# A GRU over four lanes with gathered gate rows: the candidate's input rows in a bank of their own, split products for two lanes, and the transposed embedding kept from the table stage

## The chip, the cores and the metric

The kernel runs on one core of a Trainium2 chip. The metric is the device time of the program in microseconds (us), lower is better; three runs of the kernel before took 1370.25, 1371.12 and 1375.16 us.

## What is computed

A GRU with hidden size H = 128 runs over T = 50 tokens for each of B = 2048 sequences, and the state at each sequence's last position is multiplied with the transposed embedding table (V = 12501 rows of 128), which gives the logits, 2048 x 12501 in f32.

```python
xp = jnp.einsum('bth,hk->btk', emb_table[input_ids], kernel) + b_i
rec = h @ rec_kernel + b_r
z = sigmoid(xz + rz); r = sigmoid(xr + rr)
hh = tanh(xh + r * rh)
h_new = z * h + (1.0 - z) * hh
logits = last @ emb_table.T
```

## The kernel before

**Table stage.** The product of an embedding row with the input weights depends on the token alone. So the kernel first makes a table in DRAM, `gate_table`, with 384 values (z, r and candidate parts) for each of the 12501 tokens. It goes over 24 chunks of 512 embedding rows and a rest of 213. For each chunk SyncE (SP) loads the rows into a slot of `emb_rows` (L239), TensorE (PE) turns them (L349) into `x_ps`, ScalarE (ACT) copies the high part as f32r (L528), VectorE (DVE) subtracts for the low part (L641), PE makes three f32r products for each of the four 128-row tiles (L369 to L371) into the banks of `z_ps` and `r_ps`, DVE and ACT copy them out (L650, L537), and SP stores them (L234). Each partition takes four neighbouring rows of a chunk, so that it reads 2048 and writes 6144 bytes in one piece. DVE also works out row numbers for all tokens in this stage; positions behind a sequence's last go to a row that freezes the state.

**Recurrence.** The batch is four lanes of 512 sequences. The state is kept transposed, [128 hidden, 512 sequences]. A step g takes one block (a whole lane of 512, or half of lane 3, 256 wide) through one token. There are three phases, all in groups of four steps: phase one, 100 steps on lanes 0 and 1 in turn; phase two, 100 steps, in turn a whole step on lane 2 and a half step on a half of lane 3; phase three, 50 half steps on the two halves of lane 3. Block g+2 goes on where block g ended.

GpSimd (POOL) gathers the table rows of each tile of 128 sequences with one indirect DMA (L335), four steps ahead, into the buffer that step g-4 has left. On PE a step (`step`, L409) turns the gathered rows of the r gate into `r_ps` (L399), adds the f32 product with the state (L406, two matmul instructions for one product), makes the candidate's product into `c_ps`, turns and adds for z into `z_ps`, and, after DVE has multiplied `c_ps` by r in place, adds the turned candidate rows to it. Each of the three has two banks and `x_ps` the other two. ACT (`gate`) takes r's sigmoid (L562), z's sigmoid (L564) and the candidate's tanh (L568). DVE (`update`) does (c + bias) * r in PSUM (L765), z * h (L768), (z - 1) * candidate (L772) and the new state (L775).

**What fills the gaps.** In phase one, once in four steps, SP loads a chunk of the embedding again, this time with row p of a tile on partition p (L268), PE turns it (`vocabulary`), ACT and DVE split it into `embT_hi` and `embT_lo` (L575, L780). In phases two and three every step carries two units of the logits of lanes that are done: a unit is 128 sequences by 512 vocabulary columns, three f32r products (L457, L458, L459) into one of two banks of `x_ps`. ACT copies a unit out (L586) and SP stores it. In a half step both units stand on PE behind z's product and both copies on ACT before the tanh. In a whole step the first unit stands there, the second behind the candidate's rows, and both copies behind the tanh. A unit waits until the copy of the unit before it in its bank is done (L452). At the end PE makes the units of lane 3, with ACT and DVE copying in turn (L614, L813), through `x_ps` and `z_ps`.

The order of each engine is written out by hand: four programs with `wait_ge` on counting semaphores, run in order.

Of the kernel before, what the change touches and what calls it, by code (L numbers as in the profile page):

```python
# [22 lines left out]
def gru_logits(nc, ids, mask, emb, w_in, w_rec, bias, out):  # L23
# [58 lines left out]
    def tiles_of(blk):  # L82
        return blk[2] // P
# [4 lines left out]

    def gathers(k, q):

        return sum(16 * tiles_of(phase_of(j)[q]) for j in range(k))
# [5 lines left out]
    with ExitStack() as ctx:  # L97
# [14 lines left out]
        w_rec_sb = sb("w_rec_sb", [P, G])  # L112
        bias_sb = sb("bias_sb", [P, 2, 3])
# [20 lines left out]
        z_sb, r_sb, cand = gates[:, 0], gates[:, 1], gates[:, 2]  # L134

        table_rows = gates[:].rearrange("p a b c -> p (a b c)").rearrange("p (k n g) -> p k n g", k=2, n=TPC)
        rowsT_hi = state_hi[:, 2:4]
        rowsT_lo = state_lo[:, 2:4]
# [10 lines left out]
        z_ps = psum("z_ps", [P, SETS, BANK])  # L149
        r_ps = psum("r_ps", [P, SETS, BANK])  # L150
        c_ps = psum("c_ps", [P, SETS, BANK])
        x_ps = psum("x_ps", [P, 2, CHUNK])
# [9 lines left out]
        s_w_in_parts = sem("s_w_in_parts")  # L162
        s_math = sem("s_math")
# [12 lines left out]
        s_turned = sem("s_turned")  # L176
        s_rec = sem("s_rec")
# [3 lines left out]
        s_scaled = sem("s_scaled")  # L181
        s_cand = sem("s_cand")
# [6 lines left out]
        s_rows = sem("s_rows")  # L189
        s_rowsT = sem("s_rowsT")  # L190
        s_hi = sem("s_hi")
        s_lo = sem("s_lo")
# [14 lines left out]
        def emb_chunk(chunk):  # L207

            return emb[bass.ds(chunk * CHUNK, CHUNK), :].rearrange("(n p) h -> p n h", p=P)
# [7 lines left out]
        def _(sp):  # L217
# [44 lines left out]

            sp.wait_ge(s_rowsT_ps, FULL + 1)
            for j, m in RAGGED:
                sp.dma_start(emb_rows[0:m, 0, j, :], emb[ragged_rows(j, m), :]).then_inc(s_rows, 16)
            for k in range(1, K2 - 1):
                sp.wait_ge(s_rowsT, k)
                sp.dma_start(emb_rows[:, 0], emb_chunk(k - 1)).then_inc(s_rows, 16)  # L268
            sp.wait_ge(s_rowsT, K2 - 1)
            sp.dma_start(emb_rows[:, 0], emb_chunk(K2 - 2)).then_inc(s_rows, 16)  # L270
# [39 lines left out]
        def _(pool):  # L310
# [32 lines left out]
        def _(pe):  # L343
            pe.wait_ge(s_ident, 1)

            def turn_rows(bank, slot, tiles):

                for j, m in tiles:
                    turned = nc.tensor.transpose(x_ps[:, bank, j * P:j * P + m], emb_rows[0:m, slot, j, :],  # L349
# [10 lines left out]
            def project(c, k, tiles=WHOLE, first=False):  # L360
# [487 lines left out]
```

## Time and profile before

| | us |
|---|---|
| median of 3 runs (lowest, highest) | 1371.12 (1370.25, 1375.16) |
| the profiled execution, its own time | 1370.22 |
| its span, first to last instruction | 1368.1 |
| PE busy | 1180.8 (86%) |
| POOL busy | 784.2 (57%) |
| DVE busy | 692.4 (51%) |
| ACT busy | 686.6 (50%) |

Busy time is summed over the span and says nothing of where a stage waits. The page names as the chain that ended last mostly PE's products with the state (r 12%, c 11%, z 10%) and, with 11%, "another core or an unknown queue". There is one core only: the profile says this where a semaphore rose long after the recorded end of the instruction that raises it, and other views call it "remote". Ends of matmuls are modelled.

### The profile page before, as it was taken

How to read it: one execution, taken by the hardware profiler on the slowest of the kernel's cores; microseconds unless marked ns; L12 is line 12 of the kernel's file. 1: busy time of each engine (PE TensorE's matmuls, PEld its weight loads, DVE VectorE, ACT ScalarE, POOL GpSimd, SP SyncE). 2: the span in 40 equal slices, each digit the busy share in tenths (PEclk: the TensorE clock that was granted, in tenths of full speed). 3: DMA queues.
4: the chain of work that ended last, by engine and by line, in shares of the span. 5: the costliest groups of instructions: out<-in, count | busy, mean ns of one | idle time of the engine just before them, and what ended most of it. 6: DMA issues, size and time to landing. Idle time of an engine off the chain costs nothing.

```text
span 1368.1 us, 16235 instructions
## 1 busy us (share of the span) xinstructions
PE 1180.8 (86%) x5590; PEld 795.3 (58%) x5590; DVE 692.4 (51%) x1191; ACT 686.6 (50%) x1203; POOL 784.2 (57%) x812
## 2 busy tenths in 40 slices
PE   7947778777878778778799999999999999999998
PEld 7933444343444334444466666666666668888776
DVE  7624455444545445445554555545555555444554
ACT  3522333333433333333456666666666667777644
POOL 0027667666776767667666666666666655555200
PEclk9979898888988888989999999999999999999999
DMA  8965555555555555555467887777887778888799
GB/s 292 366 179 153 142 152 146 147 152 141 154 146 148 146 154 146 148 143 159 132 196 239 260 254 253 250 238 253 256 261 253 237 249 269 285 282 284 239 365 333
DMA packets 127489, 294.21 MB, mean 215 GB/s; under 512 B 18096, under 2 KB 33456, under 8 KB 127408
## 3 DMA queue, kind: packets, MB, share of 16 engines
q0 software_dynamic: 51200, 157.34, 39.3%
q1 hardware_dynamic: 76208, 135.84, 29.6%
q8 instruction: 45, 0.74, 0.2%
q14 instruction: 36, 0.29, 0.1%
HBM read 171.30 MB, written 121.81 MB: 214 GB/s over the span
## 4 chain that ended last, share of the span: by engine, by line
PE 67%; another core or an unknown queue 11%; DVE 6%; ACT 6%; issue 5%; DMA 4%; POOL 0%; SPq 0%; DVEq 0%; ACTq 0%; POOLq 0%
PE r_ps L406 12%; PE c_ps L406 11%; PE z_ps L406 10%; PE x_ps L457 6%; PE x_ps L459 5%; PE x_ps L458 5%; PE c_ps L399 5%; PE r_ps L399 4%; PE z_ps L399 3%; DVE c_ps L765 2%; DMA gate_table<-gates 2%; ACT gates L562 2%; ACT gates L564 1%; DMA out_dram<-logits 1%
## 5 line engine op out<-in xcount | busy, mean ns | idle before, releaser
L335 POOL DMA_INDIRECT gathered<-gate_table,index x800 | 782.3, 978 | 495.9 <-issue 204.1
L564 ACT ACTIVATE gates<-z_ps,zr_bias 128x512 f32<-128x512 f32 (+1 forms) x250 | 151.6, 607 | 329.7 <-PE z_ps L406 162.7
L768 DVE TENSOR_TENSOR kept<-gates,state 128x512 f32<-128x512 f32 (+1 forms) x250 | 147.2, 589 | 237.5 <-ACT gates L564 192.0
L406 PE MATMUL r_ps<-state,w_rec_sb 128*128 128x512 f32 (+1 forms) x500 | 256.6, 598 | 0.0
L772 DVE SCALAR_TENSOR_TENSOR gates<-gates 128x512 f32<-128x512 f32 (+1 forms) x250 | 146.1, 585 | 209.0 <-issue 125.4
L399 PE MATMUL c_ps<-ident,gathered 128*128 128x128 f32 x800 | 116.4, 260 | 145.7 <-DVE c_ps L765 125.2
L406 PE MATMUL c_ps<-state,w_rec_sb 128*128 128x512 f32 (+1 forms) x500 | 235.1, 554 | 0.0
L406 PE MATMUL z_ps<-state,w_rec_sb 128*128 128x512 f32 (+1 forms) x500 | 233.8, 550 | 0.0
L399 PEld LDWEIGHTS c_ps<-ident,gathered 128*128 128x128 f32 x800 | 92.0, 144 | 232.6 <-DVE c_ps L765 180.7
L765 DVE SCALAR_TENSOR_TENSOR c_ps<-c_ps,bias_sb,gates 128x512 f32<-128x512 f32 (+1 forms) x250 | 162.0, 648 | 126.2 <-PE c_ps L406 47.2
L562 ACT ACTIVATE gates<-r_ps,zr_bias 128x512 f32<-128x512 f32 (+1 forms) x250 | 151.0, 604 | 143.3 <-PE r_ps L406 56.6
L586 ACT ACTIVATE logits<-x_ps,nan_row 128x512 f32<-128x512 f32 (+1 forms) x300 | 194.4, 683 | 20.0 <-PE x_ps L459 14.1
L568 ACT ACTIVATE gates<-c_ps,bias_sb 128x512 f32<-128x512 f32 (+1 forms) x250 | 150.3, 601 | 90.6 <-PE c_ps L399 51.8
L399 PE MATMUL z_ps<-ident,gathered 128*128 128x128 f32 x800 | 187.5, 349 | 0.0
L457 PE MATMUL x_ps<-embT_hi,state_hi 128*128 128x512 f32 (+1 forms) x350 | 176.4, 504 | 5.7 <-DVE state_lo L752 1.6
L775 DVE TENSOR_TENSOR state<-kept,gates 128x512 f32<-128x512 f32 (+1 forms) x250 | 148.6, 594 | 26.7 <-DVE gates L772 0.9
L399 PEld LDWEIGHTS z_ps<-ident,gathered 128*128 128x128 f32 x800 | 101.3, 147 | 103.6 <-issue 93.6
L406 PEld LDWEIGHTS c_ps<-state,w_rec_sb 128*128 128x128 f32 x500 | 104.1, 208 | 92.3 <-issue 86.9
L458 PE MATMUL x_ps<-embT_lo,state_hi 128*128 128x512 f32 (+1 forms) x350 | 137.1, 392 | 0.0
L459 PE MATMUL x_ps<-embT_hi,state_lo 128*128 128x512 f32 (+1 forms) x350 | 136.5, 390 | 0.0
L399 PE MATMUL r_ps<-ident,gathered 128*128 128x128 f32 x800 | 111.6, 256 | 18.7 <-DMA gathered<-gate_table,index 18.7
L399 PEld LDWEIGHTS r_ps<-ident,gathered 128*128 128x128 f32 x800 | 88.7, 145 | 26.0 <-issue 19.4
(78 smaller groups left out, 870.8 us busy)
## 6 DMA issues: line engine op xcount, KB each, us to landing
out_dram<-logits SPq DMA_DIRECT2D x192, 512.0 KB, 4.7
gate_table<-gates SPq DMA_DIRECT2D x24, 768.0 KB, 4.1
gathered<-gate_table,index POOLq DMA_INDIRECT x800
emb_rows<-in_L_rec_emb_table_dram SPq DMA_DIRECT2D x48, 256.0 KB, 4.6
out_dram<-logits SPq DMA_DIRECT2D x8, 213.0 KB, 3.9
logits<-in_r_input_ids_dram SPq DMA_DIRECT2D x1, 400.0 KB, 6.1
logits<-in_r_input_mask_dram SPq DMA_DIRECT2D x1, 400.0 KB, 6.5
gate_table<-gates SPq DMA_DIRECT2D x2, 192.0 KB, 9.2
```

Of the source, the lines that this page charges most:

```text
L335: nc.gpsimd.indirect_dma_start(gathered[:, q, n, :].bitcast(F32), None, table, bass.IndirectOffsetOnAxis(ap=index[:, g, n:n + 1], axis=0)) ...
L399: turned = nc.tensor.matmul(bank[:, n * P:(n + 1) * P].bitcast(F32R), gathered[:, q, n, gate * H:(gate + 1) * H], ident[:], is_transpose=T ...
L406: return nc.tensor.matmul(bank, w_rec_sb[:, gate * H:(gate + 1) * H], h, start=first, stop=True, skip_group_check=True)
L457: nc.tensor.matmul(bank[:, 0:even], high, embT_hi[:, bass.ds(v0, even)], start=True, stop=False)
L458: nc.tensor.matmul(bank[:, 0:even], high, embT_lo[:, bass.ds(v0, even)], start=False, stop=False)
L459: nc.tensor.matmul(bank[:, 0:even], low, embT_hi[:, bass.ds(v0, even)], start=False, stop=True).then_inc(s_unit, 1)
L562: nc.scalar.activation(r_sb[:, b, 0:width], r_ps[:, b, 0:width], ACT.Sigmoid, bias=zr_bias[:, 1:2]).then_inc(s_r, 1)
L564: nc.scalar.activation(z_sb[:, b, 0:width], z_ps[:, b, 0:width], ACT.Sigmoid, bias=zr_bias[:, 0:1]).then_inc(s_z, 1)
L568: nc.scalar.activation(cand[:, b, 0:width], c_ps[:, b, 0:width], ACT.Tanh, bias=bias_sb[:, 0, 2:3]).then_inc(s_cand, 1)
L586: nc.scalar.activation(logits[:, q * UPQ + j, 0:width], x_ps[:, j, 0:width], ACT.Identity, bias=nan_row[:, tile + j:tile + j + 1]).then_in ...
L765: nc.vector.scalar_tensor_tensor(out=c_bank, in0=c_bank, scalar=bias_sb[:, 1, 2:3], in1=r, op0=ALU.add, op1=ALU.mult).then_inc(s_scaled, 1)
L775: nc.vector.tensor_tensor(h, kept_b, new, ALU.subtract).then_inc(s_state, 1)
```

## The change

- PSUM: `r_ps` and `x_ps` have two banks each, `c_ps` and `z_ps` one each, and the units have two of their own, `u_ps`. The candidate's turned rows go to `x_ps`. DVE writes (c + bias) * r to SBUF, adds `x_ps` to it with one more operation, and ACT's tanh reads and writes SBUF.
- Order on PE in a step: r rows, candidate rows, both units, r's product, candidate's product, z rows, z's product. Order on ACT: r, z, both copies, tanh, in whole and half steps alike.
- In phases two and three each f32 product with the state becomes three f32r products (high and low parts of weights and state). DVE makes the state's parts of block g-1 within the update of block g, behind its sum. The recurrent weights are split once in the table stage.
- The table stage writes the two parts of the turned chunk straight into `embT_hi` and `embT_lo`, and phase one's second loading, turning and splitting are gone. For this a partition takes rows p, p+128, ... of a chunk: it reads 512 and writes 1536 bytes in a piece.
- POOL's gather for step g+4 waits for z's product of step g.
- The last units use `u_ps` and `r_ps`.

```diff
-            return rows[bass.ds(chunk * CHUNK, CHUNK), :].rearrange("(p n) h -> p n h", n=TPC)
+            return rows[bass.ds(chunk * CHUNK, CHUNK), :].rearrange("(n p) h -> p n h", p=P)
...
-                    pool.wait_ge(s_turned, (k - 1) * QS + q + 1)
+                    pool.wait_ge(s_z_in, (k - 1) * QS + q + 1)
...
+            def add_high(bank, high, gate, first):
+                cols = slice(gate * H, (gate + 1) * H)
+                nc.tensor.matmul(bank, w_rec_hi[:, cols], high, start=first, stop=True, skip_group_check=True)
+                return nc.tensor.matmul(bank, w_rec_lo[:, cols], high, start=False, stop=True, skip_group_check=True)
+
+            def add_low(bank, low, gate):
+                return nc.tensor.matmul(bank, w_rec_hi[:, gate * H:(gate + 1) * H], low, start=False, stop=True,
+                                        skip_group_check=True)
...
                 pe.wait_ge(s_gather[q], done)
-                pe.wait_ge(s_z, g + 1)
                 add_rows(r_bank, blk, q, 1, True)
+                if g >= SETS:
+                    pe.wait_ge(s_sum, g + 1 - SETS)
+                add_rows(x_bank, blk, q, 2, True)
+                if meanwhile is not None:
+                    meanwhile()
                 if started is not None:
                     pe.wait_ge(s_start, started)
-                if not start:
-                    pe.wait_ge(s_state, g + 1 - SETS)
-                add_state(r_bank, h, 1, False).then_inc(s_rec, 1)
-                add_state(c_bank, h, 2, True).then_inc(s_rec, 1)
-                add_rows(z_bank, blk, q, 0, True)
-                add_state(z_bank, h, 0, False).then_inc(s_z_in, 1)
-                if meanwhile is not None:
-                    meanwhile()
-                pe.wait_ge(s_scaled, g + 1)
-                add_rows(c_bank, blk, q, 2, False).then_inc(s_turned, 1)
-                if after is not None:
-                    after()
+                if k < K2:
+                    if not start:
+                        pe.wait_ge(s_state, g + 1 - SETS)
+                    add_state(r_bank, h, 1, False).then_inc(s_r_in, 1)
+                    if g > 0:
+                        pe.wait_ge(s_scaled, g)
+                    add_state(c_bank, h, 2, True).then_inc(s_c_in, 1)
+                    pe.wait_ge(s_z, g + SETS)
+                    add_rows(z_bank, blk, q, 0, True)
+                    add_state(z_bank, h, 0, False).then_inc(s_z_in, 1)
+                else:
+                    high = state_hi[:, lane, c0:c0 + width]
+                    low = state_lo[:, lane, c0:c0 + width]
+                    pe.wait_ge(s_state_hi, parts_of(g - SETS))
+                    add_high(r_bank, high, 1, False)
+                    pe.wait_ge(s_state_lo, parts_of(g - SETS))
+                    add_low(r_bank, low, 1).then_inc(s_r_in, 1)
+                    pe.wait_ge(s_scaled, g)
+                    add_high(c_bank, high, 2, True)
+                    add_low(c_bank, low, 2).then_inc(s_c_in, 1)
+                    pe.wait_ge(s_z, g + SETS)
+                    add_rows(z_bank, blk, q, 0, True)
+                    add_high(z_bank, high, 0, False)
+                    add_low(z_bank, low, 0).then_inc(s_z_in, 1)
...
-                act.wait_ge(s_turned, g + 1)
-                nc.scalar.activation(cand[:, b, 0:width], c_ps[:, b, 0:width], ACT.Tanh, bias=bias_sb[:, 0, 2:3]).then_inc(s_cand, 1)
-                if after is not None:
-                    after()
+                act.wait_ge(s_sum, g + 1)
+                nc.scalar.activation(pre[:, b, 0:width], pre[:, b, 0:width], ACT.Tanh, bias=bias_sb[:, 0, 2:3]).then_inc(s_cand, 1)
...
-                return (None, work) if tiles_of(blk) == TPL else (work, None)
+                return work
...
-                nc.vector.scalar_tensor_tensor(out=c_bank, in0=c_bank, scalar=bias_sb[:, 1, 2:3], in1=r,
+                nc.vector.scalar_tensor_tensor(out=new, in0=c_ps[:, 0:width], scalar=bias_sb[:, 1, 2:3], in1=r,
                                                op0=ALU.add, op1=ALU.mult).then_inc(s_scaled, 1)
+                dve.wait_ge(s_scaled, g + 1)
+                nc.vector.tensor_tensor(new, new, x, ALU.add).then_inc(s_sum, 1)
+                if behind is not None:
+                    state_parts(parts_of(g - 1), g - 1, behind)
                 dve.wait_ge(s_z, g + 1 + SETS)
```

Removed with it: `vocabulary`, `high_part`, `low_part`, `emb_chunk` and SP's loads at L265 to L271. After the first four steps DVE also clears the parts of lanes 2 and 3 (four more memsets).

## Rows read from the trace of the kernel before

**Rows 1.** Windows: length, busy of PE, PEld, DVE, ACT, POOL; PEclk, DMA share, GB/s.

```profile
0.00:103.00 103.00, 74.28 (x405) 68.38 (x405) 53.28 (x105) 39.46 (x79) 10.60 (x21) 0.87 0.82 279
103.00:686.00 583.00, 445.21 (x1905) 244.32 (x1904) 291.69 (x432) 210.68 (x326) 403.04 (x403) 0.88 0.52 148
686.00:1130.00 444.00, 430.84 (x2093) 293.27 (x2094) 228.76 (x404) 275.38 (x500) 283.40 (x296) 0.99 0.78 246
1130.00:1290.00 160.00, 159.83 (x888) 134.56 (x888) 79.77 (x199) 126.27 (x247) 87.17 (x92) 1.00 0.87 276
1290.00:1368.00 78.00, 70.67 (x302) 54.75 (x302) 38.91 (x56) 34.83 (x53) 0.00 (x0) 0.98 0.91 332
```

**Rows 2.** Timeline, phase one, quick stretch: start, us, what.

```profile
395.72 0.50 PE L399 MATMUL r_ps<-ident,gathered 128*128 128x128 f32 x4
...
396.05 1.09 PE L406 MATMUL r_ps<-state,w_rec_sb 128*128 128x512 f32 x2
...
399.36 0.51 PE L399 MATMUL r_ps<-ident,gathered 128*128 128x128 f32 x4
```

**Rows 3.** Timeline, phase one, slow stretch.

```profile
379.51 2.04 PE L406 MATMUL r_ps<-state,w_rec_sb 128*128 128x512 f32 x2
...
387.62 0.69 ACT L562 ACTIVATE gates<-r_ps,zr_bias 128x512 f32<-128x512 f32 x1 [2.85 <-remote]
```

**Rows 4.** Waits in 103:686, by remote: us, times, longest us.

```profile
ACT gates L564 <- remote: 101.4, 31, 5.7
...
ACT gates L562 <- remote: 43.5, 17, 4.3
```

**Rows 5.** Groups of POOL in 103:686: busy, mean ns, idle and releasers.

```profile
L335 POOL DMA_INDIRECT gathered<-gate_table,index x403 | 403.0, 1000 | 179.2 <-issue 111.1 <-remote 47.1 <-PE c_ps L399 20.9
```

**Rows 6.** Timeline, phase three, one step.

```profile
1158.88 0.66 PE L406 MATMUL z_ps<-state,w_rec_sb 128*128 128x256 f32 x2
...
1159.58 0.48 ACT L564 ACTIVATE gates<-z_ps,zr_bias 128x256 f32<-128x256 f32 x1 [0.44 <-issue]
...
1160.08 0.39 PE L457 MATMUL x_ps<-embT_hi,state_hi 128*128 128x512 f32 x1
...
1160.28 1.39 ACT L586 ACTIVATE logits<-x_ps,nan_row 128x512 f32<-128x512 f32 x2 [0.22 <-PE x_ps L459]
1160.31 0.40 PE L458 MATMUL x_ps<-embT_lo,state_hi 128*128 128x512 f32 x1
```

**Rows 7.** Timeline, phase two, half step, PE after a wait.

```profile
813.59 0.50 PE L457 MATMUL x_ps<-embT_hi,state_hi 128*128 128x512 f32 x1
...
814.36 0.49 ACT L564 ACTIVATE gates<-z_ps,zr_bias 128x256 f32<-128x256 f32 x1
814.39 0.40 PE L457 MATMUL x_ps<-embT_hi,state_hi 128*128 128x512 f32 x1
...
814.72 1.29 ACT L586 ACTIVATE logits<-x_ps,nan_row 128x512 f32<-128x512 f32 x2
```

**Rows 8.** Timeline, last half steps: narrow units, parts of the state.

```profile
1286.59 0.27 PE L457 MATMUL x_ps<-embT_hi,state_hi 128*128 128x214 f32 x1
...
1286.70 0.28 PE L458 MATMUL x_ps<-embT_lo,state_hi 128*128 128x214 f32 x1
...
1289.00 0.29 DVE L750 CAST state_hi<-state 128x256 fp32r<-128x256 f32 x1
...
1289.33 0.43 DVE L752 TENSOR_TENSOR state_lo<-state,state_hi 128x256 fp32r<-128x256 f32 x1
```

**Rows 9.** Timeline, ACT, two whole operations behind one another.

```profile
392.26 0.70 ACT L568 ACTIVATE gates<-c_ps,bias_sb 128x512 f32<-128x512 f32 x1
392.84 0.70 ACT L562 ACTIVATE gates<-r_ps,zr_bias 128x512 f32<-128x512 f32 x1
```

**Rows 10.** DMA queue q1 in 0:95: packets, MB, share of 16 engines.

```profile
q1 hardware_dynamic: 9136, 27.13, 82.8%
```

**Rows 11.** DMA queue q1 in 110:680, the second loading.

```profile
q1 hardware_dynamic: 12144, 6.03, 3.6%
```

More of the change, by code:

```diff
@@ L358, in transpose_rows, with project @@
                 turn_rows(s % 2, s, tiles).then_inc(s_rowsT_ps, 1)
-            def project(c, k, tiles=WHOLE, first=False):
+            def project(c, tiles=WHOLE, first=False):
                 pe.wait_ge(s_rowsT_lo, c + 1)
@@ L434, in landed @@
             def landed(k0, k, q):
                 return (k - (k0 - 1)) * (16 * tiles_of(phase_of(k0)[q])) + gathers(k0, q)
-            def vocabulary(n, copied, tiles):
-                def work():
-                    pe.wait_ge(s_rows, n)
-                    if copied is not None:
-                        pe.wait_ge(s_lo, copied)
-                    turn_rows(0, 0, tiles).then_inc(s_rowsT, 1)
-                return work
             def unit(tile, copies, parity, v0, width, bank):
-                if copies is None:
-                    pe.wait_ge(s_lo, FULL + 1)
-                else:
+                if copies is not None:
@@ L468, in work @@
                             pe.wait_ge(s_state_lo, parts)
[L469 to L472 removed]
+                        unit(tile + j, None if first else (k - K2) * QS + q, j, v0, width, u_ps[:, j])
+                return lambda: work((0, 1))
             for q in range(QS):
[L476 to L477 removed]
+                step(0, q, FIRST[q], landed(0, 0, q), start=(q < SETS), started=2)
             for k in range(1, K2):
                 for q in range(QS):
[L480 to L481 removed]
+                    step(k, q, FIRST[q], landed(0, k, q))
             for q in range(QS):
                 step(K2, q, SECOND[q], landed(K2, K2, q),
[L485 removed]
+                     units(K2, q, SECOND[q], q * UPQ, FULL * CHUNK, REST, first=(q == 0), parts=1 + q // 2), started=4)
             for i in range(1, K3 - K2):
@@ L493, in _ @@
                     step(i + K3, q, THIRD[q], landed(K3, i + K3, q),
-                         *units(i + K3, q, THIRD[q], lane2_tile(q), (2 * i + q // 2) * CHUNK, CHUNK,
-                                parts=3 if i == 0 and q == 0 else None))
+                         units(i + K3, q, THIRD[q], lane2_tile(q), (2 * i + q // 2) * CHUNK, CHUNK,
+                                parts=parts_of(QS * K3 - 2) if i == 0 and q == 0 else None))
             for q in range(2):
-                step(K4, q, THIRD[q], landed(K3, K4, q), *units(K4, q, THIRD[q], lane2_tile(q), FULL * CHUNK, REST))
+                step(K4, q, THIRD[q], landed(K3, K4, q), units(K4, q, THIRD[q], lane2_tile(q), FULL * CHUNK, REST))
             def last_units(i, v0, count, width, first=False):
```

180 lines of the change are left out of this document (77 added, 103 removed).

## The prediction

> **What bounds the kernel now.** I cut the span into stages first [rows 1]: the table stage to 103 us, phase one 583 us, phase two 444, phase three 160, the last units 78. That is 5.83 us for a step of phase one, 8.88 for a pair (whole and half step) of phase two, 3.26 for a step of phase three (49 intervals).
>
> Phase three is PE's: busy 159.8 of 160. Phase two nearly so: 430.8 of 444. The table stage has its DMA engines busy (0.82 over all of it), and so have the last units (0.91).
>
> Phase one is not PE's, which is busy 445 of 583 us at a granted clock of 0.88. In its quick stretches a step takes 3.64 us, from one turning of r's rows to the next [rows 2]. The four turned tiles before the r product take 0.33 us there, so twelve take 1.0, and 2.64 are left for three f32 products, 0.88 each. That the mean is 5.83 comes from slow stretches: a product that PE began at 379.51 and had streamed by 381.6 is read by ACT at 387.62 [rows 3]. Such late signals cost ACT 101 us before z's sigmoid and 43 us before r's [rows 4]. What makes them late the trace doesn't say. Below them lies POOL: 403 gathers at 1.000 us with 111 us of its own issue between them are 1.28 us each [rows 5], four to a step: 5.1 us. Phase one can't fall below 510 us.
>
> **Part one: the units' place in phases two and three.** On PE both units now stand ahead of the step's products, and the candidate's rows have left the step's end. Only r's and the candidate's rows lie between z's product and the next step's units. A unit waits for the copy of the unit before it in its bank; ACT makes the copies behind z's sigmoid; z's sigmoid waits for PE's last product of the step. So a loop closes within one step: z's product, z's sigmoid, first copy, both units, nine products, z's product. Today candidate rows, r rows and all three products lie between a half step's z and the next units, over 2 us of cover.
>
> The lengths of the loop. From z's half-width sigmoid to the first copy 0.36, 814.36 to 814.72 [rows 7]; behind a whole sigmoid 0.58, as two whole operations follow one another [rows 9]. Two copies take 1.29 [rows 7] with 0.58 between starts, so one takes 0.71 to its end. A unit on a PE that has waited takes 0.80, 813.59 to 814.39 [rows 7]; the next, at 0.23 a product [rows 6], 0.69. The second copy ends (0.58 later) before the first unit does, so it adds nothing. A product of 214 columns takes 0.11 [rows 8], of 256 columns thus 0.13. The last product of z counts with its end and the signal: z began at 1158.88 as two f32 instructions of 0.22 each, and ACT began at 1159.58, 0.25 behind the streaming [rows 6]; I take 0.2, since the recorded tail of a product (0.39 for 0.23) is 0.16.
> - Half step behind a half step: 0.36 + 0.71 + 0.04 (signal) + 0.80 + 0.69 + nine products 1.17 + z's rows 0.17 + 0.2 = 4.14 us. Phase three: 49 x 4.14 = 203 for 160, **+43 us**.
> - Whole step behind a half step: 0.36 + 0.71 + 0.04 + 0.80 + 0.69 + nine products 2.07 + rows 0.33 + 0.2 = 5.20. Half behind whole: 4.14 + 0.22 = 4.36. A pair is 9.56 for 8.88: **+34 us** over 50.
>
> What the split saves stays inside the loop. Three products of 0.23 replace an f32 one of 0.88, so a pair of phase two has 0.57 us less PE work in its whole step and some 0.2 in the half one; the sum above has it. PE alone would allow 7.6 and 3.1 us.
>
> **Part two: VectorE's additions.** In phase three DVE is busy 1.63 us a step [rows 1]; the sum adds about 0.43, the parts 0.29 and 0.43 [rows 8], together 2.8, under 4.14. In phase two 4.6 us a pair and three times as much (a whole block is two half ones) give at most 8.0, under 9.56. In phase one 2.9 and at most 0.86. The low part of block g-1 comes behind the sum of block g. That sum ends about 1.3 us behind r's product of step g; the parts take another 0.8; r's low product of step g+1 comes 4 us behind that of step g. The parts are hidden; if the loop were gone they would be late next. The tanh of step g stands behind the copies as it does now in half steps. POOL needs 12 x 1.28 = 15.4 us for two pairs, 19.1 long: hidden.
>
> **Part three: phase one.** 24 loadings, 98 turned tiles and the two splitting operations go; they stood once in four steps beside waiting engines, and I count them at nothing. What may count is slack. Today PE waits at the step's end for the product with r of the same step: behind r's product lie c, z's rows and z, 2.1 us, and the chain (signal, sigmoid 0.69 [rows 3], a multiplication of about that length) needs 1.6. Then the tanh waits for PE once more. After the change c waits for the multiplication of the step before, with z, three sets of rows and r between, 3.6 us, and the tanh needs nothing of PE. ACT hears from PE twice a step and not three times. Bounds: from above 583 (late signals of 2 to 6 us are longer than any slack; more than 583 if DVE's sum of 0.7 lies on the late chain, 25 slow stretches x 0.7 = 18), from below 510. The nearest row for a step without late signals is POOL's. I take 545, half way, **-38 us**. The four added memsets are 2 us once, beside gathers.
>
> **Part four: the table stage.** q1 moved 27.13 MB in 82.8% of 95 us, 345 GB/s while busy [rows 10], in pieces of mostly 2048 and 6144 bytes. The second loading, in pieces of 512 bytes, moved 6.03 MB in 3.6% of 570 us, 294 GB/s [rows 11]. The 6.3 MB of loads at 294 cost 3 us more. The 19 MB of stores in pieces of 1536 bytes lie between no change and that rate, +9.6 us; as they are nearer the long pieces, +4. Together **+7 us** (0 to 13). The split of the recurrent weights, about 1 us of DVE, lies beside transfers.
>
> The Trainium skill (DMA: Bandwidth & Descriptors, "Why small descriptors are slow") gives a fixed overhead of about 3 cycles for each packet beside 32-byte beats; an estimate from that is 13% on the loads and 5% on the stores, +5 us in all. The measured 294 against 345 GB/s is 17%, so the trace agrees roughly.
>
> **Sum.** Span 1368.1 + 34 + 43 - 38 + 7 = 1414; the profiled execution was 2.1 us longer than its span and the median of runs is 0.9 us above it. Forecast **1417 us**.
>
> **The rivals.**
> 1. Phase one falls to the gathers' rate, 515 us, because every late signal falls into slack. For: the slack grows by 1.5 us and the tanh is freed. Against: single waits of 4 and 5.7 us. 1417 - 30 = 1387 us. Chance 0.2.
> 2. Late signals cost in phase one what they do now. 1417 + 38 = 1455, with the sum on their chain up to 1470. Against: fewer hand-overs. Chance 0.13.
> 3. The other side: PE stays the bound of phases two and three because the loop doesn't close, units being ready early enough. Its place is the wait for the copy ahead of a unit, and it decides at 0.2 us exposed per half step, what the split saves. Then phase three takes 3.1 x 49 = 152 (-8), phase two about 8.0 a pair, DVE's load, (-44), phase one 545, the table +7: 1370 - 83 = 1288 us. Against: the orders of PE and ACT are fixed, and the wait I find is 1.05 us. Chance 0.13.
> 4. The clock falls in phases two and three. Phase one, with PE busy for 76% of the time, is granted 0.88 on the mean of its two levels (1.2 and 2.4 GHz), phase two 0.99 and three 1.00 [rows 1]; after the change PE would be busy for 79% and 75% there. PE's share of the loops is 7.2 us of a pair and 3.0 of a step; at 0.88 this adds 1.0 x 50 + 0.4 x 49 = 69 us: 1486. Against: its pauses would be 1 us and regular, those of phase one are several us. Chance 0.08. The Trainium skill (TensorE: Matmul & The Clock Gate, "A second HAM failure mode") says that frequent small pauses between groups of matmuls make the clock fall and rise again; by that rule this rival would be the likely one, by the rows it is not.
>
> **The numbers.** Forecast case 0.46, rivals 0.2, 0.13, 0.13, 0.08. The range leaves out rival 3 and rival 4, 0.21, and takes in rival 1's 1387 less 8 for the bounds, and rival 2's lower end: 1378 to 1458. A measurement of this kernel can tell about 0.5%, 7 us. Faster by more is rival 3 and a small rest, 0.14; within 0.5% the low edge of rival 1, 0.05; slower 0.81.
>
> **What would show it.** Phase three at 4.1 us a step, with PE idle for 0.7 to 1 us before the units' first product, ended by ACT's copy; phase two at 9.5 a pair; the gaps before ACT's copies ended by z's sigmoid. If PE's busy share in phase three stays near 1.00, part one is wrong. If DVE instead of ACT ends PE's waits (state parts), part two is wrong. Phase one: its length, and the "remote" waits of ACT. Table stage: the first multiplication at about 110 instead of 103 us. A phase one under 470 us, which the gather's 1.28 us forbids, would make the sign wrong.

## The result, and the profile after

The changed kernel takes **1447.7 us** (median of 4 runs, 1445.8 to 1451.9) beside 1372.0 for the kernel before (4 runs): ratio **1.055, 95% interval 1.052 to 1.059**, slower. The profiled execution took 1445.8 us with a span of 1444.0. Cut into the same stages, first the windows of the changed kernel (columns as in [rows 1]):

```profile
0.00:106.80 106.80, 74.35 (x408) 67.92 (x408) 54.15 (x107) 38.82 (x79) 10.59 (x21) 0.89 0.86 268
106.80:689.10 582.30, 429.64 (x1819) 228.82 (x1817) 344.04 (x511) 200.81 (x301) 425.51 (x404) 0.87 0.48 137
689.10:1165.90 476.80, 396.31 (x2390) 332.97 (x2391) 357.32 (x699) 280.71 (x500) 312.40 (x296) 0.99 0.74 230
1165.90:1363.40 197.50, 155.98 (x1032) 136.46 (x1030) 133.35 (x344) 122.53 (x245) 87.80 (x92) 1.00 0.70 222
1363.40:1444.00 80.60, 71.88 (x303) 54.07 (x301) 40.21 (x59) 35.60 (x54) 0.00 (x0) 0.98 0.91 321
```

The span grew by 75.9 us: table stage +3.9, phase one -0.7, phase two +32.9, phase three +37.7, the last units +2.1. PE had all of phase three before and now has 156.0 of 197.5 us. Where it waits, the timeline of one step of phase three shows (it answers to [rows 6]):

```profile
1250.00 0.28 PE L402 MATMUL r_ps<-state_hi,w_rec_hi 128*128 128x256 f32 x1
...
1251.13 0.28 PE L406 MATMUL z_ps<-state_lo,w_rec_hi 128*128 128x256 f32 x1
...
1251.45 0.48 ACT L563 ACTIVATE gates<-z_ps,zr_bias 128x256 f32<-128x256 f32 x1 [0.42 <-PE z_ps L406]
...
1251.83 1.26 ACT L577 ACTIVATE logits<-u_ps,nan_row 128x512 f32<-128x512 f32 x2
...
1252.56 0.50 PE L463 MATMUL u_ps<-embT_hi,state_hi 128*128 128x512 f32 x1 [0.85 <-ACT logits L577]
...
1253.36 0.40 PE L463 MATMUL u_ps<-embT_hi,state_hi 128*128 128x512 f32 x1
...
1254.06 0.28 PE L402 MATMUL r_ps<-state_hi,w_rec_hi 128*128 128x256 f32 x1
```

The loop, a chain of waits that comes back to where it began, can be read off: z's last product at 1251.13, its sigmoid at 1251.45, the first copy at 1251.83, then PE starts the first unit after 0.85 us of waiting, the second at 1253.36, the next step's products at 1254.06. That is 4.06 us from 1250.00. Over the phase, the group of the units' first product has this idle time ahead of it, nearly all of it ended by the copy:

```profile
L463 PE MATMUL u_ps<-embT_hi,state_hi 128*128 128x512 f32 (+1 forms) x98 | 43.4, 442 | 41.5 <-ACT logits L577 40.7 <-issue 0.8
```

Phase one kept its length. Its waits, which answer to [rows 4], and POOL's group, which answers to [rows 5], both in 106.8:689.1:

```profile
POOL gathered L325 <- issue: 115.5, 379, 0.3
ACT gates L563 <- remote: 100.6, 24, 7.8
...
DVE gates L759 <- remote: 76.7, 11, 11.9
ACT gates L561 <- remote: 76.4, 12, 10.7
```

```profile
L325 POOL DMA_INDIRECT gathered<-gate_table,index x404 | 426.0, 1054 | 156.9 <-issue 115.5 <-remote 35.9 <-PE z_ps L397 2.7
```

The signals of PE that come late are still there, fewer and longer: the two sigmoids wait 36 times for 177.0 us (48 times for 144.9 before), r's up to 10.7 us (4.3 before). POOL's row divides the stage: 426.0 us busy and 115.5 of its own issuing are 541.5 (514.1 before), and its waits for PE are 41 us (35.9, 2.7 and 2.7 in a smaller group) for 68.0 before. So POOL waited 27 us less and worked 27 us longer. Its usual gather takes 0.95 us in both kernels; what grew is the number of long ones, over 1.1 us: 118 for 60. All of these lie beside an operation of VectorE (96 gathers after and 71 before had none beside them, and none of those was long), as the second line here, of the changed kernel:

```profile
388.45 0.69 DVE L768 SCALAR_TENSOR_TENSOR gates<-gates 128x512 f32<-128x512 f32 x1
388.60 1.36 POOL L325 DMA_INDIRECT gathered<-gate_table,index  x1 [0.31 <-issue]
389.25 0.69 DVE L771 TENSOR_TENSOR state<-kept,gates 128x512 f32<-128x512 f32 x1
...
390.27 0.95 POOL L325 DMA_INDIRECT gathered<-gate_table,index  x1 [0.30 <-issue]
```

Before the table is there, q1 moves the same bytes in three times the packets (27334 for 9136, with [rows 10]), 27.02 MB in 86.7% of 100 us, 312 GB/s while busy for 345:

```profile
q1 hardware_dynamic: 27334, 27.02, 86.7%
```

### The profile page after: what moved, and what is told of

Same layout as the page of the kernel before. It is cut to its first block, busy times and chain, and to the rows that moved or that the text cites. A ratio compares the mean times of both kernels' runs of the same rounds, so it can differ in the third digit from the quotient of the medians.

```text
span 1444.0 us, 17116 instructions
## 1 busy us (share of the span) xinstructions
PE 1128.2 (78%) x5942; PEld 820.2 (57%) x5942; DVE 929.1 (64%) x1716; ACT 678.5 (47%) x1178; POOL 836.3 (58%) x812
## 4 chain that ended last, share of the span: by engine, by line
PE 41%; POOL 26%; issue 14%; DMA 7%; ACT 5%; another core or an unknown queue 3%; DVE 2%; SPq 1%; ACTq 0%; DVEq 0%; POOLq 0%
POOL gathered L325 26%; PE u_ps L463 8%; PE u_ps L464 5%; PE u_ps L465 5%; ACT logits L577 5%; DMA out_dram<-logits 3%; DMA gate_table<-gates 3%; PE z_ps L402 2%; PE z_ps L390 2%; PE z_ps L406 2%; PE r_ps L402 2%; PE r_ps L403 2%; PE r_ps L406 2%; PE c_ps L406 2%
## 5 line engine op out<-in xcount | busy, mean ns | idle before, releaser
L759 DVE SCALAR_TENSOR_TENSOR gates<-c_ps,bias_sb,gates 128x512 f32<-128x512 f32 (+1 forms) x250 | 160.7, 643 | 260.4 <-ACT gates L561 119.1
L561 ACT ACTIVATE gates<-r_ps,zr_bias 128x512 f32<-128x512 f32 (+1 forms) x250 | 150.8, 603 | 351.1 <-issue 107.6
L463 PE MATMUL u_ps<-embT_hi,state_hi 128*128 128x512 f32 (+1 forms) x350 | 153.7, 439 | 129.1 <-ACT logits L577 92.2
L577 ACT ACTIVATE logits<-u_ps,nan_row 128x512 f32<-128x512 f32 (+1 forms) x300 | 186.3, 676 | 0.0
L567 ACT ACTIVATE gates<-gates,bias_sb 128x512 f32<-128x512 f32 (+1 forms) x250 | 160.2, 641 | 27.0 <-DVE gates L762 26.0
L397 PE MATMUL c_ps<-state,w_rec_sb 128*128 128x512 f32 x200 | 117.8, 674 | 62.1 <-DVE gates L759 44.5
L762 DVE TENSOR_TENSOR gates<-gates,x_ps 128x512 f32<-128x512 f32 (+1 forms) x250 | 145.1, 580 | 8.6
L464 PE MATMUL u_ps<-embT_lo,state_hi 128*128 128x512 f32 (+1 forms) x350 | 137.3, 392 | 0.0
L465 PE MATMUL u_ps<-embT_hi,state_lo 128*128 128x512 f32 (+1 forms) x350 | 136.4, 390 | 0.0
L397 PE MATMUL r_ps<-state,w_rec_sb 128*128 128x512 f32 x200 | 123.3, 701 | 0.1
L397 PE MATMUL z_ps<-state,w_rec_sb 128*128 128x512 f32 x200 | 120.3, 686 | 0.0
```

The lines of the kernel that those rows point to most:

```text
L397: return nc.tensor.matmul(bank, w_rec_sb[:, gate * H:(gate + 1) * H], h, start=first, stop=True, skip_group_check=True)
L463: nc.tensor.matmul(bank[:, 0:even], high, embT_hi[:, bass.ds(v0, even)], start=True, stop=False)
L464: nc.tensor.matmul(bank[:, 0:even], high, embT_lo[:, bass.ds(v0, even)], start=False, stop=False)
L465: nc.tensor.matmul(bank[:, 0:even], low, embT_hi[:, bass.ds(v0, even)], start=False, stop=True).then_inc(s_unit, 1)
L561: nc.scalar.activation(r_sb[:, b, 0:width], r_ps[:, b, 0:width], ACT.Sigmoid, bias=zr_bias[:, 1:2]).then_inc(s_r, 1)
L567: nc.scalar.activation(pre[:, b, 0:width], pre[:, b, 0:width], ACT.Tanh, bias=bias_sb[:, 0, 2:3]).then_inc(s_cand, 1)
```

## The experiments

Twelve runs were made, on three chips. One plain fact is needed for their numbers: the kernel before itself takes 1288 us on the chip of e1 to e4 (called **chip A**), 1375 us on that of e5 to e8 (**chip B**) and 1386 to 1389 us on that of e9 to e12 (**chip C**), with 1372 us where the change was timed. Ratios are to the kernel before on the same chip. Stage lengths in us are from the profiled executions (table stage, phases one, two, three); "pair" and "step" are medians of whole and half step of phase two, and of a step of phase three:

| run | chip | table | one | two | three | pair | step | time | ratio (95%) |
|---|---|---|---|---|---|---|---|---|---|
| before | result's | 102.9 | 583.0 | 443.9 | 159.8 | 8.82 | 3.25 | 1372 | |
| after | result's | 106.8 | 582.3 | 476.8 | 197.5 | 9.52 | 4.06 | 1448 | 1.055 (1.052-1.059) |
| e1 | A | 107.3 | 512.8 | 423.4 | 156.1 | 8.49 | 3.18 | 1284 | 0.997 (0.994-1.000) |
| e2 | A | 106.9 | 518.5 | 400.3 | 154.3 | 7.97 | 3.17 | 1267 | 0.984 (0.972-0.995) |
| e3 | A | 107.3 | 522.9 | 472.4 | 197.5 | 9.50 | 4.06 | 1379 | 1.070 (1.066-1.075) |
| e4 | A | 106.2 | 528.9 | 415.5 | 159.8 | 8.31 | 3.25 | 1291 | 1.003 (1.002-1.005) |
| e5 | B | 107.2 | 583.9 | 475.6 | 197.5 | 9.50 | 4.06 | 1448 | 1.053 (1.049-1.057) |
| e6 | B | 107.7 | 382.0 | 476.1 | 197.5 | 9.51 | 4.06 | 1246 | 0.906 (0.902-0.909) |
| e7 | B | 102.3 | 399.8 | 443.8 | 159.8 | 8.81 | 3.25 | 1186 | 0.862 (0.859-0.866) |
| e8 | B | 107.4 | 606.0 | 460.1 | 154.4 | 8.69 | 3.16 | 1409 | 1.024 (1.019-1.029) |
| e9 | C | 106.8 | 591.9 | 472.5 | 153.9 | 8.79 | 3.16 | 1410 | 1.018 (1.015-1.021) |
| e10 | C | 107.6 | 586.4 | 474.5 | 197.5 | 9.50 | 4.06 | 1446 | 1.044 (1.040-1.048) |
| e11 | C | 107.6 | 590.8 | 477.6 | 197.5 | 9.52 | 4.06 | 1451 | 1.047 (1.043-1.052) |
| e12 | C | 112.7 | 604.2 | 481.9 | 153.9 | 9.15 | 3.16 | 1429 | 1.027 (1.022-1.033) |

**e1: both units back behind z's product, all else as changed.**

```diff
-                if meanwhile is not None:
-                    meanwhile()
...
                     add_low(z_bank, low, 0).then_inc(s_z_in, 1)
+                if meanwhile is not None:
+                    meanwhile()
```

> The changed kernel, but on TensorE both units of a step of phases two and three stand behind z's product again, as in half steps before the change; phase one is untouched. Theory (the units ahead of the products close a loop through z's sigmoid and the copies, 9.52 us a pair and 4.06 us a step): the loop opens and phase three falls to some 3.3 us a step, phase two to some 8.7 us a pair, where the chain tanh, state, next sum, state parts, r's low product ends last; in all 75 us less than the changed kernel, about 1370. Rival (VectorE's added sum and parts bound phases two and three): they keep 9.5 and 4.06 us, 1445 in all.

**e2: the units stay ahead, and ACT copies them before z's sigmoid.**

```diff
+                if meanwhile is not None:
+                    meanwhile()
                 act.wait_ge(s_z_in, g + 1)
                 nc.scalar.activation(z_sb[:, b, 0:width], z_ps[:, 0:width], ACT.Sigmoid, bias=zr_bias[:, 0:1]).then_inc(s_z, 1)
-                if meanwhile is not None:
-                    meanwhile()
```

> The changed kernel, but on ScalarE the two copies of a step stand ahead of z's sigmoid, behind r's; TensorE's order is the changed one. Theory of the loop: the units then wait only for copies that r's product releases, which leaves the loop with time to spare; phase three 3.1 us a step (TensorE's own work), phase two 7.7 to 8.0 us a pair, in all some 1315. Rival (VectorE bounds): 9.5 and 4.06 us stay, or the copies in front of z's sigmoid delay z and with it the state, 1445 or more.

Windows of e1 (phases two, three), then of e2 (phases one, two, three):

```profile
620.00:1043.00 423.00, 398.64 (x2398) 322.53 (x2397) 348.67 (x697) 299.04 (x500) 329.21 (x299) 1.00 0.84 260
1043.00:1199.00 156.00, 155.45 (x1031) 135.32 (x1030) 129.34 (x344) 127.63 (x246) 95.17 (x92) 1.00 0.88 283
```

```profile
107.00:625.00 518.00, 397.19 (x1807) 210.53 (x1807) 347.70 (x510) 198.84 (x301) 395.83 (x402) 0.98 0.54 153
625.00:1026.00 401.00, 384.87 (x2404) 327.20 (x2404) 345.81 (x699) 274.73 (x501) 308.40 (x298) 1.00 0.87 275
1026.00:1180.00 154.00, 154.00 (x1030) 136.53 (x1028) 128.65 (x343) 116.76 (x246) 87.38 (x92) 1.00 0.88 284
```

Each edit alone opens the loop: a step of phase three falls from 4.06 to 3.18 and 3.17 us, a pair from 9.5 to 8.49 and 7.97. PE is busy for all of phase three again. DVE does about as much as in the changed kernel (349 and 129 us for 357 and 133), so its added work is not what costs.

**e3: the products of phase one in two halves.**

```diff
-                return nc.tensor.matmul(bank, w_rec_sb[:, gate * H:(gate + 1) * H], h, start=first, stop=True,
-                                        skip_group_check=True)
+                for c in range(0, LANE, HALF):
+                    made = nc.tensor.matmul(bank[:, c:c + HALF], w_rec_sb[:, gate * H:(gate + 1) * H], h[:, c:c + HALF],
+                                            start=(first and c == 0), stop=True, skip_group_check=True)
+                return made
```

> The changed kernel, but each f32 product of phase one is made as two of 256 columns instead of one of 512: the same streaming, four instructions for two. Before the change phase three with 256 wide f32 products showed no late signals. Theory A (512 wide f32 products make TensorE's signals late): the late signals go and phase one falls from 582 to the gathers' rate, 510 to 530. Theory B (it is the share of f32 work or something outside TensorE, like gathers): phase one stays at 560 to 600. Phases two and three unchanged at 9.52 and 4.06 us.

It can't decide: chip A has no late signals to remove. Its use is another one: phases two and three are the changed kernel's, 472.4 and 197.5, so the loop costs the same on this chip, and 1379 is about what the change gives there.

**e4: the kernel before, with the table stored in the changed kernel's pieces.**

```diff
-            return rows[bass.ds(chunk * CHUNK, CHUNK), :].rearrange("(p n) h -> p n h", n=TPC)
+            return rows[bass.ds(chunk * CHUNK, CHUNK), :].rearrange("(n p) h -> p n h", p=P)
```

> The kernel before the change with only the mapping of rows to partitions changed, so that the table stage reads 512 and writes 1536 bytes in a piece. Theory: this alone moves the first multiplication from 102.9 to some 107 us (106.8 in the changed kernel), the rest of the kernel as before, 1375 in all. Rival: the pieces cost nothing, and the 3.9 us of the changed kernel come from elsewhere in the stage.

The first multiplication comes at 106.2 us for 102.9 (on the result's chip), +3.3; the whole takes 3.3 us more (1291.1 for 1287.8). The rest of e4 is the kernel before on chip A: phase one 529 us and not 583. POOL's group in phase one of e4, then of e2, has no idle time ended by "remote":

```profile
L335 POOL DMA_INDIRECT gathered<-gate_table,index x399 | 407.8, 1022 | 121.6 <-issue 121.3 <-PE c_ps L399 0.3
```

```profile
L325 POOL DMA_INDIRECT gathered<-gate_table,index x402 | 397.1, 988 | 122.5 <-issue 122.5
```

So phase one at 513 to 529 us is POOL without a pause. The late signals come on some chips and not on others, with either kernel. The next four kernels asked what they hang on.

**e5: the changed kernel once more, unaltered.**

> The changed kernel, unaltered, once more, on the chip of the following three runs. Theory (the units' place closes a loop through z's sigmoid and costs 0.7 us a pair and 0.8 us a step on any chip; what differs between chips is phase one alone, where signals of TensorE come late on some and not on others): where the kernel before takes 1288 us, phase one lasts 515 to 530 us, phase two 474 to 477 (9.5 a pair), phase three 197.5 (4.06 a step), the sum 1373 to 1383, ratio 1.067 to 1.074; where the kernel before takes 1372, the sum is 1445 to 1450. Rival (the change's longer slack in phase one is worth something even here, or the loop is shorter on this chip): under 1365 beside 1288.

Measured 1447.5 beside 1375.2: chip B is like the result's, and the stages agree within 1.6 us.

**e6 and e7: the changed kernel and the kernel before with three of four gathers left out in phase one.**

```diff
-        return sum(16 * tiles_of(phase_of(j)[q]) for j in range(k))
+        return sum(16 * fetched(j, q) for j in range(k))
+    def fetched(j, q):
+        return 1 if 0 < j < K2 else tiles_of(phase_of(j)[q])
...
-                for n in range(tiles_of(blk)):
+                for n in range(fetched(k, q)):
```

> The changed kernel with three of the four gathers of each block left out from the second step on in phase one (the other three tiles keep the rows of the first step, so a part of the computation is left out; PE, ACT, DVE do the same work on the same sizes). POOL then needs 1.3 us a step. Theory (without late signals the gathers' 1.28 us each bound phase one): phase one falls from some 520 us to PE's own rate, 3.65 to 3.9 us a step, 365 to 390 us, and the whole by 130 to 155 us, to 1225 to 1250 beside 1378. Rival A (a chain of ACT and DVE bounds phase one): 4.5 us a step or more, 450 us, the whole 1310. Rival B, where late signals show in this run (waits of ACT ended by PE with a remote signal of several us): they come from PE's f32 products and not from the gathers' traffic, and phase one stays at 550 us or more.

> The kernel before with the same three of four gathers left out in phase one. It tells what the change does to phase one's other limits. Theory of the prediction (PE waits for the gate with r of the same step, but its slack of 0.5 us holds while signals come in time): 3.7 us a step, 370 to 385 us, the same as the changed kernel, and the whole at 1288 - 145 = 1143 (1130 to 1160). Rival (the same step's gate and the tanh cost PE some tenths of a us each step, hidden by the gathers): 4.1 us a step or more, 410 us, 1185.

Windows of phase one, e6 and then e7:

```profile
107.70:489.70 382.00, 370.44 (x1810) 214.55 (x1809) 340.00 (x511) 200.94 (x300) 111.67 (x115) 0.99 0.22 61
```

```profile
102.30:502.10 399.80, 389.21 (x1906) 220.38 (x1904) 284.80 (x432) 208.62 (x325) 125.81 (x116) 0.99 0.25 73
```

The late signals all but vanish (ACT has one of 4.2 us in e6 for 43 in e5, 190 us), phase one falls by 202 us, its median step is 3.66 us, and the clock is 0.99 for 0.86. By an estimate, 512 - 382 = 130 us of these are what 400 gathers at 1.28 us took beyond PE's own pace, and the other 72 what the late signals cost. Where the gathers don't bound, the changed kernel is 18 us quicker (3.66 for 3.94 us a step). That isn't slack: PE's idle time is 11.6 us in e6 and 10.6 in e7, and its busy time is 370.4 for 389.2. Most of this is the turning of the second loading, 15 us, which the change takes out (e7, phase one):

```profile
L353 PE MATMUL x_ps<-ident,emb_rows 128*128 128x128 f32 x97 | 14.7, 273 | 0.0
```

Phase one of e7, 399.8 us, lies between its two expectations (370 to 385, and 410).

**e8: e2, with split products in phase one too.** In step() the branch of lanes 2 and 3 is taken for all (parts_of(g) returns g + 1), and DVE makes state_hi and state_lo behind every sum.

> The changed kernel with ACT's copies ahead of z's sigmoid, and with the split products of lanes 2 and 3 taken for lanes 0 and 1 as well, so phase one has no f32 product of the state: nine products of 0.23 us instead of three of 0.88, and two more operations of DVE a step. Theory (the gathers bound phase one on a chip whose signals come in time): phase one stays at 515 to 525 us although PE loses 0.57 us a step, phase two 400, phase three 154, the sum 1260 to 1270. Rival (PE's f32 products hold back z's signal and through it the next gather, which waits for it): phase one under 505 us. On a chip with late signals: if f32 products cause them, phase one falls from 583 to 530 or less; if not, it stays over 560.

Phase one took 606 us with no f32 product of the state in it: these products are not the cause.

**e9: e2 once more, on chip C.**

> The changed kernel with ACT's copies ahead of z's sigmoid, as in the run of that name before, for an interval and for its time where TensorE's signals come late. Theory (the order of copies and z's sigmoid is all that closes the loop; late signals come when POOL issues gathers back to back, and this variant's quick pairs of 7.97 us leave POOL only 0.3 us of rest a pair): where the kernel before takes 1288 us, 1260 to 1268 (ratio 0.984). Where it takes 1372, phase three is 154 to 155 us, phase two 445 to 465 as in the run with split products everywhere, phase one 575 to 590, the sum 1375 to 1400. Rival (in phase two late signals came from the split of phase one alone): phase two 400 to 415, sum 1325 to 1340.

Windows of its phases one and two:

```profile
106.80:698.70 591.90, 434.44 (x1811) 232.64 (x1809) 344.84 (x511) 200.00 (x302) 420.23 (x404) 0.85 0.47 135
698.70:1171.20 472.50, 415.73 (x2399) 339.95 (x2398) 351.12 (x698) 275.12 (x500) 302.98 (x296) 0.94 0.74 233
```

Phase two, 400.3 us on chip A, took 472.5, a little over what was expected, and pairs of 7.5 us stand beside pairs of 12 and 14. With PE's loop open POOL is again without rest (6 gathers x 1.28 = 7.7 of 7.97 us), and the late signals come into phase two; in e5, with pairs of 9.5, there was one, of 3.8 us. What e2 wins on chip A is lost here: 1.018.

**e10 and e11: one step less lead for POOL; and a third of the bytes.** Both on the changed kernel, against its 583 us of phase one.

```diff
-                    pool.wait_ge(s_z_in, (k - 1) * QS + q + 1)
+                    pool.wait_ge(s_z_in, (k - 1) * QS + q + 2)
```

```diff
-                        gathered[:, q, n, :].bitcast(F32), None, table,
+                        gathered[:, q, n, 0:G if (k == 0 or k >= K2) else H].bitcast(F32), None,
+                        table if (k == 0 or k >= K2) else table.rearrange("r (a b) -> (r a) b", b=H),
```

> The changed kernel in which each gather waits for z's product of one step later than it must, so that POOL can run three steps ahead at most, not four. All work is kept. Theory A (late signals last as long as POOL can go on issuing gathers without a pause, and end when it runs into its own wait): with one step less of lead the longest waits shrink by about 5 us, phase one falls from 583 to 530 to 560 us, the sum to 1395 to 1425 where the kernel before takes 1372. Theory B (late signals have nothing to do with POOL's lead): phase one 575 to 595, sum 1447. Where the kernel before takes 1288, phase one is bound by the gathers at 515 to 525 either way, since 7.3 us of PE's work lie between the signal and the rows' use, against 5.1 of gathers and 1.8 to land; sum 1378.

> The changed kernel with gathers of phase one, from its second step on, that fetch 512 bytes a row instead of 1536, from other places of the table (so a part of the computation is changed); POOL issues as many gathers as before. Theory A (late signals come with POOL's issuing of gathers): phase one stays within 570 to 590 us where the kernel before takes 1372, the sum 1440 to 1450. Theory B (they come with the traffic of the gathers): a third of the bytes, the waits go, and phase one falls to POOL's rate, 505 to 525 us, the sum 1370 to 1390. Where the kernel before takes 1288 it only tells whether POOL's 1.28 us a gather depend on the bytes: if not, 510 to 525.

e10's theory A fell: 586.4 us. In e11 traffic went from 137 to 50 GB/s and phase one stayed at 590.8 with the same waits (POOL 50.3 us by "remote"): it is the number of gathers that counts, not their bytes. POOL's group in phase one, e10 and e11:

```profile
L325 POOL DMA_INDIRECT gathered<-gate_table,index x401 | 418.6, 1044 | 165.7 <-issue 112.3 <-remote 48.5 <-PE z_ps L397 4.9
```

```profile
L325 POOL DMA_INDIRECT gathered<-gate_table,index x403 | 416.3, 1033 | 170.9 <-issue 114.6 <-remote 50.3 <-PE z_ps L398 6.0
```

**e12: more work for PE, so that POOL should get pauses.** On e9:

```diff
-                add_rows(r_bank, blk, q, 1, True)
+                for _ in range(6 if k < K2 // 2 else 7 if k < K2 else 2 if k < K2 + K2 // 2 else 3 if k < K3 else 1):
+                    add_rows(r_bank, blk, q, 1, True)
```

> The changed kernel with ACT's copies ahead of z's sigmoid (e9), in which PE turns r's rows several times over before the r product, into the same bank: 5 extra turnings of 0.33 us in each of the first 48 steps of phase one, 6 in the other 52; in phase two one extra in the first 24 pairs, two in the last 26 (0.5 us a pair each, whole and half block together). The result is the same; PE only does more. It makes a step of phase one 5.3 and then 5.65 us of PE's own work, against 5.1 of POOL's gathers, and a pair of phase two 8.5 and then 9.0 against 7.7. Theory 1 (late signals appear only where POOL issues gathers back to back; a PE slower than POOL leaves it pauses, and they go): phase one falls from e9's 592 to 550 to 570 us although PE works 167 us more, the second half of it evenly at 5.6 to 5.75 us a step, and phase two from 472 to 440 to 450, at 8.5 to 8.7 and 9.0 a pair; the sum 1355 to 1375 beside 1372 to 1386 of the kernel before. Theory 2 (this chip takes a gather each 1.46 us on the mean, whatever else runs, and the late signals are how that limit shows): phase one 583 to 600, both halves at 5.83 or more, phase two 445 to 455, the sum 1385 to 1410. Theory 3 (late signals come at random in any step): phase one at 5.33 and 5.65 plus the 2 us a step that they cost now, 750 us. Where the kernel before takes 1288 us: phase one 550, phase two 438, the sum 1330, by any theory.

Phase one took 604.2 us, and evenly: behind its first group 6.0 us a step in the first part as in the second, though PE's own work differs by 0.33. Theories 1 and 3 fell. Theory 2 had the two equal halves right and the sizes wrong: 604.2 for 583 to 600, and 481.9 for 445 to 455 in phase two (10.0 us a pair in its first part, 9.3 in its last). POOL's group, and two stretches of the timeline that show what repeats every 12 us:

```profile
L325 POOL DMA_INDIRECT gathered<-gate_table,index x398 | 410.8, 1032 | 188.9 <-issue 106.8 <-remote 75.7 <-PE z_ps L397 6.5
```

```profile
497.86 1.72 PE L390 MATMUL r_ps<-ident,gathered 128*128 128x128 f32 x14
497.89 0.95 POOL L325 DMA_INDIRECT gathered<-gate_table,index  x1 [0.30 <-issue]
...
500.01 1.38 PE L390 MATMUL r_ps<-ident,gathered 128*128 128x128 f32 x14 [0.43 <-issue]
500.10 0.69 ACT L562 ACTIVATE gates<-r_ps,zr_bias 128x512 f32<-128x512 f32 x1 [5.31 <-remote]
500.45 0.94 POOL L325 DMA_INDIRECT gathered<-gate_table,index  x1 [1.62 <-remote]
...
512.02 0.78 PE L390 MATMUL r_ps<-ident,gathered 128*128 128x128 f32 x7 [0.49 <-issue]
512.13 0.69 ACT L562 ACTIVATE gates<-r_ps,zr_bias 128x512 f32<-128x512 f32 x1 [5.33 <-remote]
512.48 0.95 POOL L325 DMA_INDIRECT gathered<-gate_table,index  x1 [1.64 <-remote]
```

POOL stops for 1.6 us, since PE's signal for its buffer isn't there. Then PE (which had paused in the middle of 28 turnings, with no wait between them), ACT and POOL all go on within 0.45 us. Phase one has 49 pauses of POOL over 1.2 us; in 46 of them ACT starts 0.35 us before POOL does, and in 43 PE goes on 0.4 to 0.5 us before. So in this run the signals of PE, to ACT and to POOL, come together, about 1.2 us after POOL has stopped issuing; POOL stops because the signal that it needs is one of them. Eight gathers and one such pause are 8 x 1.03 + 7 x 0.3 + 1.6 = 11.9 us for two steps, whatever PE does.

e5 has a place of the same kind with a longer hold (timeline, chip B):

```profile
384.12 1.12 PE L397 MATMUL r_ps<-state,w_rec_sb 128*128 128x512 f32 x2
...
389.44 0.95 POOL L325 DMA_INDIRECT gathered<-gate_table,index  x1 [0.30 <-issue]
...
393.84 0.69 ACT L561 ACTIVATE gates<-r_ps,zr_bias 128x512 f32<-128x512 f32 x1 [11.32 <-remote]
394.19 0.94 POOL L325 DMA_INDIRECT gathered<-gate_table,index  x1 [3.80 <-remote]
```

r's product ends at 385.24, POOL goes on until 390.39, ACT gets the signal at 393.84, and POOL, again 0.35 us later, the signal of a z product that had ended at 383.42 by the trace.

**What stays open.** That PE's signals wait for POOL is read from their common release in e12, from e6 and e7 (few gathers, hardly a late signal) and e11 (bytes don't matter). It is not shown to be the whole cause. Of ACT's late waits over 1.5 us, 47 of 50 end in a pause of POOL in e12, but only 12 of 34 in the changed kernel and 15 of 37 in e5; the others end while POOL still issues. The low clock is not the cause: phase one of e12 was granted 0.99, and ACT waited 252 us there for r's products alone. Whether only the signals are held or PE itself is, the trace can't tell: the ends of its products are modelled, and in e12 PE stood still for some 0.4 us in the middle of its turnings. Why a chip does this and another doesn't no run tells, and no kernel was tried that gathers without POOL.

## Why the prediction was right, and where it was wrong

The sign, the range and the forecast's case were right: 1447.7 in 1378 to 1458, for a forecast of 1417. In span, +76 us for +46.

- **Part one, the loop: right.** 4.14 us a step was worked out and 4.06 measured, 9.56 a pair and 9.52. Term by term in the row of a step: sigmoid to copy 0.38 (0.36 taken), copy to unit 0.73 (0.71 + 0.04), first unit 0.80, second 0.70 (0.69), nine products, z's rows and the hand-over 1.45 (1.54). +37.7 us for +43 and +32.9 for +34. e1 and e2 show that it is this loop: either end of it opened, and it is gone.
- **Part two, DVE hidden: right.** DVE is busy 133 us in phase three (2.7 a step, 2.8 estimated), and e1 and e2 keep it at that without the cost.
- **Part three, phase one: wrong, and this is the step that failed.** "I take 545, half way, -38 us" measured -0.7. The prediction took POOL's 1.28 us a gather as a floor at 510 that the change leaves alone, and what lay above it as late signals that slack could shorten. The waits did shrink: [rows 5] has 68.0 us in which POOL waited for PE (47.1 and 20.9), and after the change they are 41, 27 less. But POOL's own work, which the prediction carried over unchanged, grew from 514.1 to 541.5 us, 27 more. e5 repeats it: 49.3 us of waits, 532.4 of its own work. What makes the long gathers is not shown. They lie beside operations of VectorE, which got 52 us more of them, but on chip A they did not grow in number (58 in e4; 30, 45 and 68 in e1 to e3). Nor do the runs tell whether the gain and the loss are one thing: with all gathers kept, phase one took 582 to 606 us in all eight profiles outside chip A, whatever was changed. The part that was counted at nothing, the second loading's turnings, is worth 15 us of PE's time, which shows only where the gathers are gone (e6, e7). Putting -0.7 for -38 turns 1417 into 1454, within 7 us of the result.
- **Part four, table stage: right in sign, oversized.** +3.9 for +7 (0 to 13). The same bytes moved at 312 GB/s while busy for 345, and e4 gives +3.3 for the short pieces alone, loads and stores together. The Trainium skill's rule (DMA: Bandwidth & Descriptors, "Why small descriptors are slow") gave an estimate of +5: the trace agrees in sign and roughly in size (+3.9, and +3.3 in e4).
- **Rival 2** (late signals cost in phase one what they do now, 1455, chance 0.13) has the length of phase one right, though not what makes it up; it deserved more than rival 1. The 513 to 523 us on chip A are not rival 1's 515: the stage is short there for the kernel before too (529 in e4). **Rival 3** (the loop doesn't close) is disproved by its own row: a wait of 0.85 us instead of under 0.2. Its numbers for an open loop were good: 152 and 400 us forecast, 154.3 and 400.3 in e2 on chip A; on chip C e9 has 153.9 and 472.5.
- **Rival 4, the clock: fell.** Phase two was granted 0.99 and phase three 1.00, the level of 2.4 GHz nearly throughout, with PE busy for 83% and 79% of them and a pause of 0.85 us in every step. The Trainium skill (TensorE: Matmul & The Clock Gate, "A second HAM failure mode") would have it fall; the measurement differs and decides. In the changed kernel's recurrence the clock fell almost only in phase one (0.87), and before each of its 23 falls there PE had paused for 1.6 to 10.2 us; it was 0.98 to 0.99 in phase one of e2, e4 and e6, which have hardly a late signal.

**No version beats both kernels everywhere.** e2, one statement moved, is quicker than the changed kernel, for which e3 stands on chip A (1267 beside 1379) and e10 on chip C (1410 beside 1446). It beats the kernel before on chip A alone (0.984), and loses on chip C (1.018), where a quicker phase two only brings the late signals into it.

## What to carry to other kernels

Before work is moved on one engine, write the loop that it closes, with the other engines' fixed order in it, and add up its members from rows: here that gave 4.14 us for 4.06, while the busy shares spoke of a gain. Take the idle time of each engine in a stage apart by what ended it. Here POOL's own work made 514 of 583 us and the rest were waits for PE, so it was on the path; its work has to be priced anew for the changed kernel, and not carried over, before slack elsewhere is counted as a gain. And time a change of this size on more than one chip: one edit was 1.6% quicker on one and 1.8% slower on another.

## What was not expected of the hardware

- The same kernel took 1288 us on one chip and 1372 to 1389 wherever else it ran; the difference is phase one (529 and 583 us, with e4 for chip A) and phase two (415.5 and 444).
- On the chips of the longer time, signals of TensorE reach ACT up to 11 us late while POOL issues gathers one behind another. In e12 PE, ACT and POOL then go on together, about 1.2 us after POOL stops, in 43 of 49 pauses; in the other runs most late signals don't keep to this. With a quarter of the gathers they are all but gone; with a third of the bytes they aren't.
- No gather without an operation of VectorE beside it took over 1.1 us (0.95 us each, 167 of them in phase one of the two kernels); with one beside it 60 of 332 did before and 118 of 308 after.
- A gather of 128 rows took POOL the same whether its rows had 1536 or 512 bytes: 1.04 (e10) and 1.03 us (e11), with 0.3 between two.
